# Attention exponentials: two neighbouring score banks of a head in one ScalarE instruction of 1024 columns

## The reference, cut to what matters

```python
qkv = (x @ w_qkv).reshape(B, L, 3, H, Dh)            # B=4, L=1024, H=16, Dh=8
attn = jnp.einsum('bhid,bhjd->bhij', q, k) * scale
attn = attn + phi_bias(L)[None, None]
attn = jax.nn.softmax(attn, axis=-1)
out = jnp.einsum('bhij,bhjd->bhid', attn, v)
out = jnp.transpose(out, (0, 2, 1, 3)).reshape(B, L, D)
return out @ w_proj + b_proj
```

## Time and profile before

| what | value |
|---|---|
| time, median of 3 runs | 1076.78 us (1076.03 to 1079.19) |
| profiled execution: span, first to last instruction | 1086.9 us (the page gives no other time of it) |
| mean granted TensorE clock | 0.962 of full speed |
| PE / DVE / ACT / POOL busy over the span | 90% / 84% / 67% / 34% |
| exponentials on ScalarE (L1349) | 1024, 553.1 us busy, 598 ns each |

### The profile page before, as it was taken

How to read it: one execution, slowest core, us unless ns; L and a number is a source line. 1 busy time by engine, 2 the same in 40 slices (tenths; PEclk the granted TensorE clock), 3 DMA queues, 4 the chain that set the end, 5 groups by cost and what they waited for, 6 DMA issues and landing times. The chain is left out here.

```text
span 1086.9 us, 36163 instructions
## 1 busy us (share of the span) xinstructions
PE 973.5 (90%) x11666; PEld 545.0 (50%) x11667; DVE 912.1 (84%) x1795; ACT 726.6 (67%) x1574; POOL 367.8 (34%) x481
## 2 busy tenths in 40 slices
PE   5549997778999999999999999999999997649998
PEld 4549997432333333333333333333333345649997
DVE  7558886679999999999999999999999976548886
ACT  1124443557888888888888888888888874224443
POOL 2624443212223233232232232332323244534444
PEclk9999999787999999999999999999999999569999
DMA  9722221773422122222222222222222434722221
GB/s 302 259 76 72 63 68 31 203 254 104 136 77 76 57 74 73 60 72 72 61 72 71 61 73 70 66 71 67 67 73 64 120 95 144 272 79 67 68 65 34
DMA packets 83933, 105.65 MB, mean 97 GB/s; under 512 B 15835, under 2 KB 67041, under 8 KB 83344
## 3 DMA queue, kind: packets, MB, share of 16 engines
q1 hardware_dynamic: 75888, 90.10, 27.8%
q0 software_dynamic: 5568, 12.63, 3.4%
q10 hardware_dynamic: 2432, 2.36, 0.6%
HBM read 74.14 MB, written 35.50 MB: 101 GB/s over the span
## 5 line engine op out<-in xcount | busy, mean ns | idle before, releaser
L1213 DVE TENSOR_REDUCE nmax<-psS 128x1 f32<-128x1024 f32 x507 | 595.3, 1218 | 37.1 <-PE psS L1057 28.9
L1349 ACT ACTIVATE big<-psE 128x512 f32<-128x512 f32 x1024 | 553.1, 598 | 91.1 <-PE psE L1042 88.6
L1042 PE MATMUL psE<-qop,kop 122*32 122x512 bf16 x4096 | 317.9, 384 | 4.9 <-ACT big L1349 3.4
L1423 POOL TENSOR_TENSOR big<-big,const 128x512 f32<-128x512 f32 x128 | 163.2, 1275 | 441.5 <-ACT big L1349 441.5
L1077 PE MATMUL psV<-big,vst 128*9 128x256 f32 x4096 | 265.5, 379 | 1.3
L1057 PE MATMUL psS<-maxop 32*128 32x512 bf16 x1014 | 173.6, 390 | 21.0 <-DVE nmax L1213 13.1
L1077 PEld LDWEIGHTS psV<-big,vst 128*9 128x9 f32 x4096 | 101.7, 90 | 116.3 <-issue 12.8
L1042 PEld LDWEIGHTS psE<-qop,kop 122*32 122x32 bf16 x4096 | 90.4, 95 | 130.7 <-ACT big L1349 59.4
L1057 PEld LDWEIGHTS psS<-maxop 32*128 32x128 bf16 x1014 | 47.7, 91 | 178.7 <-issue 109.0
L789 ACT ACTIVATE siga<-psGa,w1sa 128x128 f32<-128x128 f32 x156 | 44.5, 368 | 62.2 <-PE psGa L701 62.2
L789 ACT ACTIVATE sigb<-psGb,w1sb 128x128 f32<-128x128 f32 x156 | 44.5, 368 | 62.1 <-PE psGb L701 62.1
(11 more groups left out here) (194 smaller groups left out, 933.8 us busy)
## 6 DMA issues: line engine op xcount, KB each, us to landing
maxop<-qk_parts SPq DMA_DIRECT2D x256, 64.0 KB, 1.9
qop<-qk_parts SPq DMA_DIRECT2D x64, 144.0 KB
kop<-qk_parts SPq DMA_DIRECT2D x64, 144.0 KB
weighted_sums<-osum SPq DMA_DIRECT2D x64, 128.0 KB
xs<-sorted_a SPq DMA_DIRECT2D x39, 128.5 KB, 2.0
xs<-sorted_b SPq DMA_DIRECT2D x39, 128.5 KB
qk_parts<-big SPq DMA_DIRECT2D x12, 384.0 KB, 3.2
w1a<-in_w SPq DMA_DIRECT2D x1, 4128.0 KB
```

Of the source, the lines that this page charges most:

```text
L1042: last = nc.tensor.matmul(psE[BANK[turn]][32 * c:32 * c + 32, :], kop[b][0:TROWS, lo:lo + 32], qop[b][0:TROWS, half * HALF:(half + 1) * HALF],
L1213: nc.vector.tensor_reduce(nmax[r % 2][:, qt:qt + 1], psS[n % 2][:], AX.XY, ALU.max, negate=True).then_inc(s_max, 1)
L1349: nc.scalar.activation(prob[r % 2][:, lo:lo + HALF], psE[BANK[16 * (r % NBUF) + n]][:], ACT.Exp).then_inc(s_exp, 1)
L1423: nc.gpsimd.tensor_tensor(dst, dst, diag[:, 4 * h:4 * h + 4, :], ALU.mult).then_inc(s_diag, 1)
```

## The change

The three psE banks become one PSUM tensor of three banks that lie side by side. Where a turn has bank 0 and the next turn of the same head has bank 1 (`joined`), ScalarE waits until both turns' matmuls are done, computes both in one instruction of 1024 columns and raises `s_exp` by 2 at its end. The other turns keep their own instruction of 512 columns. TensorE's order and the counts that it waits for stay as they were.

```diff
-        psE = [m.ps(f"psE{s}", [P, HALF]) for s in range(3)]
+        scores = m.ps("psE", [P, 3, HALF])
+        psE = [scores[:, s, :] for s in range(3)]
...
+        def joined(turn):
+
+            return BANK[turn] == 0 and turn % 16 != 15
...
                 for n in range(16):
-                    if live(at, 0):
-                        act.wait_ge(s_t, 16 * i + n + 1)
+                    turn = 16 * (r % NBUF) + n
+                    if live(at, 0) and not (n and joined(turn - 1)):
+                        wide = 2 if joined(turn) else 1
+                        act.wait_ge(s_t, 16 * i + n + wide)
...
-                        kt, half = n // 2, n % 2
-                        lo = kt * PBLK + half * HALF
-                        nc.scalar.activation(prob[r % 2][:, lo:lo + HALF], psE[BANK[16 * (r % NBUF) + n]][:],
-                                             ACT.Exp).then_inc(s_exp, 1)
+                        lo, bank = n * HALF, BANK[turn]
+                        nc.scalar.activation(prob[r % 2][:, lo:lo + wide * HALF].rearrange("p (w q) -> p w q", q=HALF),
+                                             scores[:, bank:bank + wide, :], ACT.Exp).then_inc(s_exp, wide)
```

More of the change, by code:

```diff
@@ L1041, in weigh @@
                             lo = kt * P + 32 * c
-                            last = nc.tensor.matmul(psE[BANK[turn]][32 * c:32 * c + 32, :],
+                            last = nc.tensor.matmul(psE[BANK[turn]][32 * c:32 * c + 32],
                                                     kop[b][0:TROWS, lo:lo + 32],
```

## The result

The changed kernel takes 1163.14 us (1160.85 to 1164.16), 1.079 times the time before (95% interval 1.0773 to 1.0812): 85 us slower where 62 were forecast, inside the range and near its upper end, 1167.

A forecast was written before the change was run, and what follows sets the result against it. The bound was VectorE's loop of maxima with TensorE's pieces, 10.10 us a head. TensorE's chain of 38.2 plus 6.1 of stops in four heads gave 11.09 a head, 1077 + 62 = 1139 us, range 1123 to 1167.

The forecast's parts named there:

- What bounds the kernel: Attention heads: VectorE's maxima and TensorE's pieces form a loop of 5.01 us per half head; ScalarE is outside it.
- The bank goes back later: psE banks: turn t+3 must wait for the whole pair (t, t+1), costing 0.99 us a head.
- the step of the bank: From the start of a pair's second turn to its bank's next turn: at least 0.44 + 1.01 + 0.05 = 1.50 us.
- upper bound, 1164: Whole program, if a pair takes 1.09 us: stops of 0.50 and 0.27, +1.39 us a head, 1164 us.
- The chain without waits: TensorE's own pieces: quarters of 1.08 + 1.31 us, 9.56 us a head, 38.2 in four heads.
- the stops: TensorE in front of a bank: ten of 0.42 and ten of 0.19 us, 6.1 us in four heads.
- Score waits: Rival: VectorE's loop keeps its 0.54 us a head beside the stops, 11.63 a head, 1173 us; chance 0.06.
- Two whole records: Rival: a pair's exponential takes 1.20 us with nothing overlapped, +1.93 us a head, 1199 us; chance 0.05.
- The clock: Rival: TensorE's pauses lower its clock, 55 us more per tenth of heads, at least 1194 us; chance 0.03.
- Banks one by one: Rival: the pair releases bank 0 halfway, 1.09 us against 1.08, and the time stays at 1077; chance 0.03.
- Faster: Rival: ScalarE sets the pace, so its saving of 0.4 us a head counts, 1052 us; chance 0.03.

The follow-up runs named there:

- experiment 8: The kernel before, without pairs, with every exponential of the loop computing only 256 of its 512 columns: 1074.4 us, 0.997 times the kernel before.
- experiment 7: The changed kernel, with each pair in the loop's 56 heads computing only 256 columns of each bank: 1090.4 us, 1.012 times the kernel before.
- 3 and 4: The changed kernel with half the pairs joined: only those with a gather before the bank's next turn, 1101.6 us; only those with scores there, 1120.9 us.
- experiment 1: The changed kernel, with every exponential instruction raising s_exp by 1 and waits counting instructions: 1144.2 us, 1.061 times the kernel before.
- experiment 6: The changed kernel, with the copy of psV ahead of the pair in heads that begin with one: 1156.2 us, 1.074 times the kernel before.
- experiment 2: The changed kernel, still waiting for both turns but reading the banks with two single exponentials: 1104.6 us, 1.024 times the kernel before.
- experiment 5: The changed kernel, with two single exponentials after the joint wait and the copy of psV between them: 1095.2 us, 1.017 times the kernel before.

## Why the prediction held, and where it was off

*What bounds the kernel.* Right: ScalarE was not in the loop (experiment 8), and its saving counted for nothing.

*The bank goes back later.* Right, and shown: the loss is in heads of 11.41 us, `weigh` waits for ScalarE, and shortening the pair alone takes nearly all of it away (experiment 7; a faster ScalarE without pairs gives only 0.3%, experiment 8). That a pair's price is the step of the bank less what TensorE does meanwhile is borne out by 3 and 4.

*The size of that step* is the term that was mis-sized. It was put together as 0.44 + 1.01 + 0.05 = 1.50, and measured 1.58. The pair took 1.024, 0.427 more than a single one, 0.834 ns a column; the copies of 128 and 512 columns gave 0.79 and misled by 0.014. The start took 0.50, not 0.44: I carried the start of an exponential whose wait is its own over to one whose wait is a separate instruction, and the diff's count of 2 was the sign of it. Twenty pairs by 0.08 are 1.6 us in four heads, 0.4 a head, more than the whole difference from 11.09 to 11.41. The prediction's upper bound, 1164, has a step of 1.58 too, but from a pair of 1.09 us; that the measured 1163 lies beside it is luck. With a count of 1 the pairs cost 65 us (experiment 1), close to the 62 of the forecast. The Trainium skill, page "ScalarE: Activation LUTs", section "What ACT_TABLE_LOAD costs", states 0.833 ns a column, and the measured 0.834 agrees; its whole estimate of 1.04 for a pair was as far off on the other side.

*The chain without waits.* The 1.08 across the scores "where nothing waits" held a wait: in the earlier trace rows the second score starts 0.22 after the first, at 511.37, just as VectorE is done with its buffer (506.57 + 4.74 = 511.31 in the earlier trace rows). The second score's two matmuls alone:

```profile
511.37 0.39 PE L1057 MATMUL psS<-maxop 32*128 32x512 bf16 x2
```

After the change, with both buffers free, four matmuls of a score pair end 0.40 after the first began, so they start together. A chain without waits is shorter than 9.56 a head, by up to 0.22 for each quarter. It entered the sum on both sides: the stops are longer, and the steps that are not stopped are shorter. The 20 steps of pairs are 10 x 1.08 + 10 x 1.31 = 23.9 us of the chain of 38.2 by the prediction's numbers, which left 14.3 for the other turns of four heads. In the trace of the change, eighteen of the twenty steps are 1.57 to 1.59, one is 1.65, and one is 1.90, where the copy of psV holds up ScalarE ahead of the pair. They add up to 32.0 of the 45.6, which leaves 13.7 for the others.

*The copy of psV* was left out. It stands behind the pair in every fourth head and held up the gather; in experiment 6 moving it was worth 4 us by those heads and 7 by the whole time. The prediction named what stands behind the stopped turn on TensorE, and did not name what stands behind the pair on ScalarE.

*The rivals.* Score waits: they did not add up with the stops; VectorE's 82.6 us of idle time show that it is now ahead. Two whole records: a pair is 1.024, not 1.20. The clock stayed at 1.00 with TensorE 88% busy and stops of up to 0.64 us. What the page "TensorE: Matmul & The Clock Gate" of the Trainium skill (section "A second HAM failure mode: psum-queue depth-cycling") describes showed in no run here. Banks one by one: experiment 2 comes nearest to it, and 25 us of the cost stay. The prediction counted for this rival only the first bank's return, 1.09; the second bank, which is back after 1.58, is what TensorE mostly waits for (experiment 5). Faster: experiment 8 excludes it.

## What to carry to other kernels

Before joining two instructions that drain a buffer, follow the buffer, not the engine: the first half waits for the second to be filled and goes back only with it. With three banks in rotation the producer then has one bank to work on; compare the time from the second fill to the joint return with the time in which the producer comes round again, and do it for both buffers: with the joint wait alone, and the two read one by one, it was the second that came back late. An engine that mostly waits has nothing to gain from fewer instructions. And look at what the joined instruction carries: a count other than one can cost it its own wait, and whatever stood between its halves now stands behind both.

## What the runs showed of the chip

An exponential from PSUM takes 382, 597 and 1024 ns for 256, 512 and 1024 columns. A pair whose count is 2 starts 0.06 us later after its matmuls than one whose count is 1, which over 320 pairs made 19 us. The two scores of a quarter, four matmuls on 32 rows each, run side by side when both of their buffers are free: the four took 0.40 us in all, where a second score with its buffer late made them 0.61 to 0.85.
